# Softmax exponentials head by head on ScalarE, square sums by side, and a new order of work in a six-layer attention block

## The reference

```
q, k, v = split(shift(x) @ Wqkv)            # 16 heads of 64
q, k = l2norm(q) * qs, l2norm(k) * ks ; rotary embedding on both
sim  = 8 * q . k over this window of 32 and the one before  # 64 keys, masked
out  = softmax(sim) @ v ; x = out @ Wo + x
x    = (a * gelu(gate)) @ W2 + x            # a, gate = layernorm(shift(x)) @ W1 + b1
```

## Time and profile before

| | |
|---|---|
| median of 3 runs | 1942.52 us (1942.41 to 1943.18) |
| profiled execution, its own time | 1940.85 us |
| its span | 1939.1 us |
| mean granted TensorE clock | 0.977 of full |
| PE / DVE / ACT / POOL busy | 90% / 74% / 59% / 41% |
| chain that ended last | PE 60%, DVE 22%, POOL 6%, issue 4%, ACT 4% |

### The profile page before, as it was taken

One profiled execution on the slowest core, in us unless ns is written; L12 is line 12 of the kernel. 1 busy time (PEld: TensorE's weight loads), 2 busy tenths in 40 slices (PEclk: granted clock), 3 DMA queues, 4 the chain that ended last, 5 costly groups with the idle time before them and its releaser, 6 DMA issues.

```text
span 1939.1 us, 80741 instructions
## 1 busy us (share of the span) xinstructions
PE 1742.4 (90%) x35952; PEld 1405.9 (73%) x35952; DVE 1436.7 (74%) x2083; ACT 1142.3 (59%) x2065; POOL 791.5 (41%) x612
## 2 busy tenths in 40 slices
PE   6568999999899998999988999998998999999996
PEld 5247777777777777777777777777777777777775
DVE  6757768867877876887786688777778768868863
ACT  2035666666656665666665666666566666656653
POOL 1024434544443453443363344355434444534430
PEclk9679999999999999999999999999999999999998
DMA  3067565566556556646546664656665556555551
GB/s 99 1 148 167 132 143 131 121 145 163 124 136 142 121 126 174 146 113 140 135 118 160 143 145 111 139 142 153 142 146 122 127 140 142 125 139 137 116 126 40
DMA packets 98316, 252.93 MB, mean 130 GB/s; under 512 B 29872, under 2 KB 36144, under 8 KB 97200
## 3 DMA queue, kind: packets, MB, share of 16 engines
q1 hardware_dynamic: 97968, 247.76, 54.0%
HBM read 44.23 MB, written 2.10 MB: 24 GB/s over the span
## 4 chain that ended last, share of the span: by engine, by line
PE 60%; DVE 22%; POOL 6%; issue 4%; ACT 4%; DMA 2%; SPq 2%; POOLq 0%; DVEq 0%
PE ps L356 53%; PE ps L534 6%; DVE UV L729 5%; DVE mx L796 4%; POOL E L1111 4%; DVE E L790 4%; DVE zl L841 4%; ACT E L874 2%; SPq L317 1%; POOL Qtb L1101 1%; DMA rope<-in_c_rope 1%; DVE R L758 1%; ACT zr L874 1%; DVE sq L710 1%; PE ps L498 0%
## 5 line engine op out<-in xcount | busy, mean ns | idle before, releaser
L729 DVE SCALAR_TENSOR_TENSOR UV<-ps,veca,rope 128x512 f32<-128x512 f32 x768 | 523.4, 744 | 74.8 <-PE ps L356 59.5
L1101 POOL TENSOR_TENSOR Kt<-UV 128x512 f32<-128x512 f32 x192 | 242.5, 1284 | 587.4 <-DVE UV L729 587.4
L874 ACT ACTIVATE sq<-ps 128x512 f32<-128x512 f32 (+1 forms) x400 | 232.8, 582 | 274.9 <-PE ps L356 206.7
L1101 POOL TENSOR_TENSOR Qtb<-UV 128x512 f32<-128x512 f32 x192 | 241.7, 1281 | 161.8 <-DVE UV L729 161.8
L1111 POOL TENSOR_TENSOR E<-E,mx 128x1024 f32<-128x1024 f32 x96 | 182.9, 1905 | 304.1 <-DVE mx L796 296.2
L356 PE MATMUL ps<-xh,wh 128*128 128x256 f32 x768 | 238.6, 311 | 5.4 <-ACT sq L874 4.1
L356 PE MATMUL ps<-xl,wh 128*128 128x256 f32 x768 | 218.3, 284 | 3.0 <-issue 2.8
L356 PE MATMUL ps<-xh,wl 128*128 128x256 f32 x768 | 218.6, 285 | 0.4 <-issue 0.4
L356 PE MATMUL ps<-Kb,Qtb 64*32 64x64 f32 (+1 forms) x12288 | 186.5, 222 | 26.3 <-issue 25.9
L874 ACT ACTIVATE OT<-ps 128x512 f32<-128x512 f32 x192 | 104.2, 595 | 170.7 <-PE ps L534 170.2
L356 PEld LDWEIGHTS ps<-Kb,Qtb 64*32 64x32 f32 x12288 | 156.6, 106 | 52.4 <-issue 51.7
(11 more groups left out here) (132 smaller groups left out, 3746.6 us busy)
## 6 DMA issues: line engine op xcount, KB each, us to landing
V<-Vs SPq DMA_DIRECT2D x672, 128.0 KB
Kb<-Kt SPq DMA_DIRECT2D x384, 128.0 KB
Qtb<-Qtb SPq DMA_DIRECT2D x384, 128.0 KB, 2.4
rope<-in_c_rope SPq DMA_DIRECT2D x48, 512.0 KB
raw<-in_Wqkv SPq DMA_DIRECT2D x6, 1536.0 KB, 7.0
V<-Vs SPq DMA_DIRECT2D x96, 64.0 KB
V<-V SPq DMA_DIRECT2D x96, 64.0 KB, 2.0
wo<-in_Wo SPq DMA_DIRECT2D x6, 512.0 KB
```

Of the source, the lines that this page charges most:

```text
L729: e.scalar_tensor_tensor(UV[:, p % 2, slot, :].rearrange("p (i t) -> p i t", i=2), ps[:, half, :].rearrange("p (i t) -> p i t", i=2), veca ...
L874: return e.activation(out, in_, f, **kw)
L1101: e.tensor_tensor(dst, u, v, op).then_inc(s["rot_done"], 1)
```

## The change

- b_sub is gone. b_max writes the negated maximum (mx), and b_exp is 16 activations of 128x64, one per head, each with one column of mx as bias and one column of rs as accumulated output. b_sum keeps only the reciprocal.
- a_norm is called twice a round instead of four times, once for k and once for q, with eight float32 matmuls that go over all four column tiles for each half; a_sqy, a_rck and b_rcq count accordingly.
- c_zh is two activations on ACT (add the bias in place, then round), and c_zl moves from DVE to POOL as a plain subtraction.
- SCHEDULE has another order throughout. The mask's own matmuls are as before.

```diff
-SCHEDULE = """b_lnq b_rcq a_rot0 a_vs0 a_vs1 a_sqy0 a_sqx0 b_sub0 a_v0 b_rq c_wo a_v1 a_xs+1 b_rqt a_rl c_xs a_x0 a_sqy1
...
+SCHEDULE = """a_v0 a_v1 b_rcq a_rot0 a_x0 a_rot1 a_vs0 a_mx0 a_y0 a_vs1 b_s0 c_wo a_my0 c_xb a_xs+1 a_sqy0 a_xh+1 b_lnq
+    a_sqx0 c_xs c_zsq b_rqt b_rq a_sqy1 a_x1 a_sqx1 c_rs b_s1 a_mx1 b_exp0 a_lnk a_sqy2 b_scale0 b_pto0 c_zh c_zl
+    c_mu b_max0 a_my1 a_rl a_y1 a_rck a_rh a_sqx2 c_var b_s2 c_zn a_rot2 b_exp1 a_norm0 b_scale1 b_s3 a_x2 b_max1
+    c_gelu0 b_pto1 a_mx2 a_halo a_my2 a_y2 b_pt0 b_att0 c_gelu1 b_sum0 a_sqy3 a_kn0 a_sqx3 w_h0 b_div0 b_att1
+    a_sp0 a_kn1 c_gelu2 b_oto0 a_rot3 c_wh a_sp1 c_h0 c_hm0 a_x3 b_pt1 a_y3 a_mx3 c_h1 b_att2 w_l0 b_ot0 a_xl+1
+    c_h2 a_norm1 c_hm1 a_my3 w_h1 c_down b_att3 w_l1 b_wo c_hm2 w_l2 c_wl c_fin w_h2 b_sum1 b_div1 b_xb b_oto1
+    b_ot1""".split()
...
-            def a_norm(m, p):
+            def a_norm(m, side):
+                e.wait_ge(s["sq_done"], m * 8 + 4 * side + 4)
...
                 for half in range(2):
-                    for i in range(2):
+                    for q in range(HQ):
+                        ins = mm(ps[q * W:(q + 1) * W, NORM, side * T:(side + 1) * T], ind[:, :],
+                                 sq[:, q // 2, half, q % 2 * T:(q % 2 + 1) * T], half == 0, half == 1,
+                                 tile_position=(0, q * W))
...
-                e.tensor_reduce(mx[:, c], heads(E[:, c]), AX.X, ALU.max).then_inc(s["m_done"], 1)
+                e.tensor_reduce(mx[:, c], heads(E[:, c]), AX.X, ALU.max, negate=True).then_inc(s["m_done"], 1)
...
-                e.tensor_reduce(rs[:, c], heads(E[:, c]), AX.X, ALU.add).then_inc(s["rs_done"], 1)
...
             def b_exp(n, c):
-                e.wait_ge(s["sub_done"], n * C + c + 1)
-                act(E[:, c], E[:, c], ACT.Exp).then_inc(s["p_done"], 1)
+                e.wait_ge(s["m_done"], n * C + c + 1)
+                ev = E[:, c].rearrange("p j r k -> p (j r) k")
+                for h in range(H):
+                    ins = act(ev[:, h, :], ev[:, h, :], ACT.Exp, bias=mx[:, c, h:h + 1], accum_out=rs[:, c, h:h + 1])
+                ins.then_inc(s["p_done"], 1)
...
             def c_zh(j, _):
                 e.wait_ge(s["zn_done"], j + 1)
-                act(zh[:, :], zs[:, :], ACT.Identity, bias=vecc[:, j // G % 2, LB:LB + 1]).then_inc(s["zh_done"], 1)
+                act(zs[:, :], zs[:, :], ACT.Identity, bias=vecc[:, j // G % 2, LB:LB + 1]).then_inc(s["zb_done"], 1)
+                e.wait_ge(s["zb_done"], j + 1)
+                act(zh[:, :], zs[:, :]).then_inc(s["zh_done"], 1)
...
+            def c_zl(j, _):
+                e.wait_ge(s["zh_done"], j + 1)
+                e.tensor_tensor(zl[:, :], zs[:, :], zh[:, :], ALU.subtract).then_inc(s["zl_done"], 1)
```

More of the change, by code:

```diff
@@ L219, in program @@
             vproj_done vs_done v2_in v2_halo k_in q_in proj_done sq_done mul_done rot_done norm_done rc_done ln_done r_done
-            rh_done rl_done rkb_done khat_done k_halo rqt_done rq_done s_done e_done m_done sub_done p_done rs_done
+            rh_done rl_done rkb_done khat_done k_halo rqt_done rq_done s_done e_done m_done p_done
             ri_done pt_done pts_done o_done on_done ot_done ots_done wo_done xb_done cb_done z_act mu_done
-            zsq_done var_done zln_done rstd_done zn_done zh_done zl_done h_done gelu_done hm_done w2_done
+            zsq_done var_done zln_done rstd_done zn_done zb_done zh_done zl_done h_done gelu_done hm_done w2_done
             fin_done fin_sum""".split()
@@ L465, in a_y @@
                 project(m, p, 1)
-            def a_norm(m, p):
-                e.wait_ge(s["sq_done"], m * 8 + 2 * p + 2)
-                if p == 2:
+            def a_norm(m, side):
+                e.wait_ge(s["sq_done"], m * 8 + 4 * side + 4)
+                if side:
                     e.wait_ge(s["rc_done"], m * 2 + 1)
-                elif p == 0 and m:
+                elif m:
                     e.wait_ge(s["rq_done"], m)
                 for half in range(2):
-                    for i in range(2):
-                        q = 2 * (p % 2) + i
-                        ins = mm(ps[q * W:(q + 1) * W, NORM, p // 2 * T:(p // 2 + 1) * T], ind[:, :],
-                                 sq[:, p % 2, half, i * T:(i + 1) * T], half == 0, half == 1, tile_position=(0, q * W))
+                    for q in range(HQ):
+                        ins = mm(ps[q * W:(q + 1) * W, NORM, side * T:(side + 1) * T], ind[:, :],
+                                 sq[:, q // 2, half, q % 2 * T:(q % 2 + 1) * T], half == 0, half == 1,
+                                 tile_position=(0, q * W))
                 ins.then_inc(s["norm_done"], 1)
@@ L751, in clamp @@
             def clamp(step, side):
-                e.wait_ge(s["norm_done"], step * 4 + 2 * side + 2)
+                e.wait_ge(s["norm_done"], step * 2 + side + 1)
                 if step and side == 0:
@@ L795, in b_max @@
                 e.wait_ge(s["e_done"], n * C + c + 1)
-                e.tensor_reduce(mx[:, c], heads(E[:, c]), AX.X, ALU.max).then_inc(s["m_done"], 1)
+                e.tensor_reduce(mx[:, c], heads(E[:, c]), AX.X, ALU.max, negate=True).then_inc(s["m_done"], 1)
             def b_sum(n, c):
                 e.wait_ge(s["p_done"], n * C + c + 1)
-                e.tensor_reduce(rs[:, c], heads(E[:, c]), AX.X, ALU.add).then_inc(s["rs_done"], 1)
-                e.wait_ge(s["rs_done"], n * C + c + 1)
                 e.reciprocal(ri[:, c].rearrange("p j r -> p (j r)"), rs[:, c]).then_inc(s["ri_done"], 1)
@@ L837, in c_zn @@
                                        ALU.mult).then_inc(s["zn_done"], 1)
[L839 to L842, removed]
             def c_hm(j, i):
@@ L868, in _ @@
                  "b_max": b_max, "b_sum": b_sum, "b_div": b_div, "b_xb": b_xb, "c_xb": c_xb, "c_zn": c_zn,
-                 "c_zl": c_zl, "c_hm": c_hm, "c_fin": c_fin}, tail)
+                 "c_hm": c_hm, "c_fin": c_fin}, tail)
         @block.scalar
@@ L967, in a_sqy @@
                 if m or p >= 2:
-                    e.wait_ge(s["norm_done"], m * 4 + p - 1)
+                    e.wait_ge(s["norm_done"], m * 2 + p // 2)
                 act(sq[:, p % 2, 1, :], ps[:, 1, :], ACT.Square).then_inc(s["sq_done"], 1)
@@ L1106, in a_rl @@
                 e.tensor_tensor(Rl[:, :], R[:, 0, :], Rh[:, :], ALU.subtract).then_inc(s["rl_done"], 1)
[L1108 to L1113, removed]
+            def c_zl(j, _):
+                e.wait_ge(s["zh_done"], j + 1)
+                e.tensor_tensor(zl[:, :], zs[:, :], zh[:, :], ALU.subtract).then_inc(s["zl_done"], 1)
+            run({"w_l": w_l, "c_wl": c_wl, "c_zl": c_zl, "a_xl": a_xl, "a_halo": a_halo, "a_rot": a_rot, "a_rl": a_rl},
                 lambda g: None)
```

## The result

The changed kernel takes 2115.89 us (median of 4 runs, 2113.89 to 2118.23) against 1942.47 us: ratio 1.0891, 95% interval 1.0872 to 1.0910. The forecast was 2175 us in a range of 2010 to 2370, slower with 0.88. The direction and the mechanism held; the size was 59 us too high, and one thing that I had called worthless was not.

What follows compares the result with a forecast made beforehand. PE's own work was taken to bound the kernel. The new round summed to 41.6 us against 36.77; 48 x 4.83 = 232 on 1940.85 gave about 2173 us, 2175 against the median, range 2010 to 2370.

Steps and rivals of the forecast that it cites:

- t: Price of one 128x64 exponential in b_exp, with bias and accumulated sum: 0.35 us, its readout overlapping; chance 0.50.
- The three stretches: The new round followed from a_sqy1's start to y1's end: 30.4 + 32t us, 41.6 in all.
- ACT's run: First stretch, on ACT without a gap from a_sqy1's start to c_gelu0's end: 8.25 + 32t us.
- To the next a_v0: Second stretch, from c_gelu0's end to the next a_v0 on PE: 10.4 us.
- To the next y1: Third stretch, from a_v0 to y1's end: 11.8 us.
- What bounds before: PE's own work sets the round, busy 34.61 of 36.77 us; its longest gap is 0.97 us.
- PE's waits: PE waits nearly 8 us a round in the changed kernel, before pt0, att0 and pt1.
- The square sums: a_norm on PE takes 2 x 1.16 us in place of 3.14, a gain of 0.8 us a round.
- DVE and POOL: DVE loses 4.3 us a round, POOL two subtractions of 1.905; neither sets the round, so worth nothing by themselves.
- A free readout: Rival for b_exp: the readout is free or hidden, t = 0.25, a round of 38.4 us, about 2020 us; chance 0.16.
- No overlap: Rival for b_exp: t between 0.42 and 0.55, rounds of 43.8 to 48.0 us, 2280 to 2480 us; chance 0.22.
- The break-even of 0.20: Value of t at b_exp, in us; rival: t falls below it, PE bounds again, 1865 us at 0.15; chance 0.08.

## Why the prediction was right, and where it was not

The edits can be laid out in a row of three kernels: before 1.0000; with square sums and zl 0.9522; with the new order as well 0.9980; with the new softmax as well 1.0891. That is -93, +89 and +177 us. Each step holds only after the one before it: the order is bad for the old softmax and good for the new one.

- **b_exp.** Right in kind, and the sum made of the right pieces: a readout of its own that overlaps. t was taken at 0.35, it is 0.331: 32 x 0.019 = 0.6 us a round, 29 of the 59 us.
- **The three stretches.** ACT's run: 8.25 + 32 x 0.331 = 18.8, measured 1224.85 - 1206.49 = 18.4. To the next a_v0: 10.4, measured 1234.98 - 1224.85 = 10.1. To the next y1: 11.8, measured 11.7. Together 0.8 us too much, 38 us; in ACT's run it is c_rs, a_lnk, c_zh and a_rh, 2.85 us where the forecast had 3.3. Against that the spans differ by 175 us and 48 x 3.43 is 165. The other 10 us are not even: the first c_fin comes 12.7 us later, the 45 rounds behind it are 3.3 us longer each, since the rounds of a new layer grew less than the others, and the last two take 13.9 more.
- **What bounds before.** "So PE's own work sets the round" was half of it: the chain that ended last leaves PE for zl, b_scale1, b_max1, b_sub1 and b_exp1, a stretch that the 0.97 us of PE's longest gap did not show.
- **PE's waits.** Nearly 8 us a round in three places: where the clock stays at full, PE is busy 33.6 of 40.2 us, so it is 6.6, less than the forecast's 7.8 mostly because the round is 1.4 shorter. The three waits are 2.2, 1.2 and 1.6 us; usually the third is filled by work at half clock. I had not foreseen that the clock would fall.
- **The square sums.** 0.8 us a round, measured 0.96 on the kernel before. The term is short by 0.16 us, because a group of sixteen costs 1.00 us to the next start where a group like b_s3 follows at once (1208.18 to 1209.18 in the changed kernel), not 1.16.
- **DVE and POOL.** This step failed: "both are worth nothing by themselves". It was read off busy shares (DVE 28.2 of 36.8 us), although the row of zl, 1.93 us for what takes 0.48 elsewhere, stood in the evidence. zl alone was worth 50 us in the old order. It did not spoil the sum, since the new order was followed with zl already moved, and DVE is 5% of its chain; no run has the new order with zl on DVE.
- **The order.** I followed it for the new softmax only and never asked what it would do to the old one, so "the only gain on the engine that bounds" hid a gain of 93 us and a loss of 89.
- **The range.** Its upper end was to be t = 0.47, but the sum gives about 2359 us there, not 2370; nothing hangs on it.
- **The rivals.** A free readout (t 0.25) is excluded by its own record and by the run without it. No overlap (0.42 and more) is excluded by the starts. The break-even of 0.20 was not reached even without bias or without sum (0.24 each).

How much of the 89 us of the new order is the wait for b_sub0, how much the queues of DVE and POOL and how much ACT's behind b_exp0 was not separated. What makes the "issue" waits that lengthen some rounds is open too.

## What to carry to other kernels

Price a loop of small activations by the distance of their starts, piece by piece (fixed part, bias, readout), and multiply by their number before anything else: splitting one instruction into 16 saved one VectorE sum and one GpSimd subtraction and cost four times its own length on top. Then ask which block lies beside other work of the waiting engine; here the first block cost twice what the second did. An instruction that takes four times what its shape takes elsewhere is worth a look even on an engine with slack, since others stand behind it: follow the chain that ended last round the loop, not only the busiest engine. And before filling a wait to hold the clock up, look where the next long wait stands.

## What the runs showed of the hardware

- An accumulated output of ACT is a second record, ACTIVATION_READ_ACCUMULATOR, 189 ns long; it adds 0.092 us to the distance of starts. A bias from memory adds 0.091 us and is not hidden back to back.
- TensorE's granted clock was 1.00 in the round of before with one wait of 0.97 us, and fell to 0.50 behind waits of 2.22 and 1.21 us in nearly every round of the changed kernel, for 3.4 or 6.8 us in most. With the first wait filled it stayed at full there and fell behind the wait of 1.66 us for b_exp1 in 23 of 45 rounds. It costs nothing beside a longer run of ACT and some 0.8 us where PE is on the chain.
- A VectorE instruction on two SBUF tensors (zl, 128x256) took 2.02 us when started 0.17 us behind a GpSimd subtraction of 1.90 us, and 0.48 us alone.
- Float32 square sums: 16 records over four column tiles take as long as 8 over two, 1.07 or 1.08 against 1.06 us, whether they come from one call or from two that stand together.
